# Output tiles 0 to 3 of an attention and FFN kernel emitted in another order

## The chip, the cores and the metric

The kernel runs on all 8 cores of one Trainium2 chip, each core on two of the 16 sequences, with no exchange between cores. The time is device microseconds of the slowest core, and smaller is better. Engines: PE does matrix products, DVE elementwise work and statistics, ACT the exponentials, POOL (GpSimd) elementwise work in SBUF, SP issues DMAs. Each takes its instructions strictly in the order in which the program gave them out.

## What is computed

```python
# x: (16, 2048, 1024); 16 heads of 64
x = x + ln(attn(ln(x)))     # q = xWq; k = (xWk)Wl; v = (xWv)Wl; softmax(q k^T / 8) v; then Wo, bo
x = x + ln(ffn(ln(x)))
def ffn(x):                 # base + shared low rank + routed low rank
    base = x @ base_W.T + base_b
    shared = (x @ shared_A.T) @ shared_B.T                    # rank 16
    gate = softmax(x @ router_W.T + router_b)                 # 6 experts, top 2, renormalised
    h = einsum('bsi,eri->bser', x, routed_A)
    routed = einsum('bser,eor,bse->bso', h, routed_B, sparse(gate))
    return base + shared + routed
```

## The kernel before

A core's work is one main loop of 512 steps m (`for m in range(NM)`, below `def rate_of`). A step issues two score blocks (`qk(2m)`, `qk(2m+1)`), then a portion of side work for PE from the list `filler`, then the two products of the probabilities with v of the step before (`pv`). ACT makes one exponential of 128x1024 for each score block. Steps 0 to 255 are the attention of sequence 0, 256 to 511 that of sequence 1. Four steps make a unit: at its end, in steps divisible by four, DVE gets a reciprocal (L1171) and a product (L1183).

`filler` is a flat list of (cost, function, ready). One cost unit is about one 128x128 by 512 matmul. The list is taken strictly from its head. In each step `credit` grows by `rate` and is capped at 1.6 times the rate; items are issued while credit is positive and the head's `ready` holds. An item that isn't ready holds back everything behind it, and what credit goes beyond the cap is lost. For m below 256 the rate is 6.03 units (1,496 units in 248 steps); from 256 on it is what is left of the list divided by the steps up to m = 481, about 4.5 to 4.6.

The input projections of both sequences fill the list up to m = 247. Then come the 32 output tiles of 128 rows. A tile n has these links:

- `tr_u(n)` (2 units): 8 PE transpositions of the attention output into a PSUM bank `fb`, and one DVE copy to `ut` (L251).
- `z_group(n, h)`, h = 0, 1 (8 units each): the product with Wo. At the end of each half DVE adds the bias (L812) and takes statistics (L257); after h = 1 also L261, and POOL runs the chain of `norm_add`: three operations on 128x1 (L266 to L268), a scale of 128x1024 (L277), an add of 128x1024 (L793).
- `ln3(n)` (no PE work), not before 3 steps after z: two DVE statistics and L261, which need POOL's add, then on POOL L266 to L268 and the scale into `xn` (L277).
- `tr3(n)` (2 units), not before 3 steps after `ln3`: 8 transpositions (L853) and a DVE copy to `x3fm`.
- `h_group(n)` (1.84 units): the low-rank product with the router's columns. DVE copies it to `hs` (L868), adds the router's bias (L870), takes the maximum; two steps later ACT takes the exponentials.
- `gate_a(n)`, `gate_b(n)`: DVE alone, six and six small operations (L890 to L896, L903 to L910).
- `tr_h(n)` (0.25 unit): one transposition (L924) of the gated `hm`, and a copy.
- `y_group(n, h)` (9 units each): the FFN's product, with DVE and POOL work at its end as for z (L946, L257, L261, then POOL's chain and the store).

So a tile is some 40 units. The filler matmuls have two PSUM banks, handed out by `next_bank`:

```python
if len(ring["list"]) == 2 and not big:
    return ring["list"][ring["n"] % 2]
b = ring["list"][ring["n"] % len(ring["list"])]
ring["n"] += 1
```

A half of z or y is `big` and moves the ring on. A transposition or an `h_group` is not: it takes the bank that the next half will get, and leaves the ring as it is. Each group waits on PE, before its first matmul, until DVE has emptied its bank (`bfree`). For `h_group` that is the copy L868, for a transposition the copy L251.

The order of the tiles is written out in the loop `for n in range(NT - 2)` (L992). In the pass for tile n, `tr_u(n+1)` and `gate_a(n-2)` lie inside z(n, 0), `tr3(n-1)` and `gate_b(n-2)` inside z(n, 1), then y(n-2) with `tr_h(n-2)` and `h_group(n-1)` inside its first half and `ln3(n)` inside its second. For n = 0 and 1 there is no y. Tiles 28 to 31 have an order of their own.

Of the kernel before, what the change touches and what calls it, by code (L numbers as in the profile page):

```python
# [70 lines left out]
def build_nc():  # L71
# [17 lines left out]
    with ExitStack() as ctx:  # L89
# [503 lines left out]
        def add(fn, cost=0.0, ready=None):  # L593
            filler.append((cost, fn, ready))
# [6 lines left out]
        def past(name, dm):  # L601

            return lambda: state["tail"] or name in mark and clock["m"] >= mark[name] + dm

        def held(group, ready):
            return [(group[0][0], group[0][1], ready)] + group[1:]
# [143 lines left out]
        def u_ready(n):  # L750
            if n >= NT - 2:
                return n in u_last and clock["m"] >= u_last[n][1] + 1
            return (n // 2 in u_tok and len(u_tok[n // 2][1]) == (8 if n < 16 else 1)
                    and clock["m"] >= u_tok[n // 2][2] + 1)

        def load_u(n):

            if n < NSEQ * 16 - 2:
                seq, t = tile_of(n)
                done_at(("l", n))  # L760
                u_ld[n] = P.dma("Y", qur[n % 2], urow[n % 2][:], u_scr[seq, t], u_tok[n // 2][1],
                                urow_free[n % 2], fb_tok["a1"])
# [44 lines left out]
        def z_group(n, h):  # L807
            s, xs = n % 2, n % 4

            def evict(pa, tok):  # L810
                o = x2[xs][:, h * 512:(h + 1) * 512]
                ev = P.op("V", lambda v: v.tensor_tensor(o, pa, bo_t[:, h * 512:(h + 1) * 512], ALU.add),  # L812
                          tok, bo_evs, x2_free[xs] if h == 0 else None, fb_tok["a1"])
                a = ln_stats("z", n % 4, h, o, ev)
                if h == 1:
                    u_free[s] = tok
                    ag = ln_aggr("z", n % 4, a)
                    slot, xt = res[n]

                    def done(tok2, half):  # L820
                        z_out[n] = xload["free"][slot] = tok2
                        if half is not None:
                            z_half.append(tok2)
                    norm_add(n, "z", x2[xs], xst[slot], ag, done, xt)
                    done_at(("z", n))
                return ev
            return late_group(512, lambda k: ut[s][:, k, :], lambda k: wo_sb[:, k, h * 512:(h + 1) * 512],
                              NCH, evict, lambda: [ut_tok[n], w_tok["wo"]])
# [4 lines left out]
        def ln3(n):  # L833
            xs, s = n % 4, n % 2
            done_at(("x", n))
            ln_stats("x", n % 4, 0, x2[xs][:, 0:512], z_half[0] if n == NT - 1 else z_out[n])
            a = ln_stats("x", n % 4, 1, x2[xs][:, 512:1024], z_out[n])
            ag = ln_aggr("x", n % 4, a)
            rt = ln_rstd("x", n % 4, ag)
            xn3_tok[n] = ln_apply("S" if n == NT - 1 else "G", "x", n % 4, xn3[s][:], x2[xs][:], rt, xn3_free[s],  # L840
                                  fb_tok["a1"])
# [131 lines left out]
        def t3_of(n):  # L973
            return [(2.0, lambda: tr3(n), past(("x", n), 3))]

        def h_of(n):
            return held(h_group(n), past(("t", n), 1))

        def th_of(n):
            return [(0.25, lambda: tr_h(n), past(("gb", n), 1))]  # L980
# [8 lines left out]
            else:  # L989
                add(lambda: gate_b(n), 0.0, past(("ga", n), 1))  # L990

        for n in range(NT - 2):  # L992
            tu = [(2.0, lambda n=n: tr_u(n + 1), past(("l", n + 1), 2))] if n + 1 < NT - 2 else []
            z0 = held(z_group(n, 0), past(("u", n), 1))
            filler += z0[:4] + ([] if late(n + 1) else tu) + z0[4:6]
            if n > 1:
                gates(n - 2, 0)
            filler += z0[6:]
            if n + 2 < NT - 3:
                if not late(n + 2):  # L1000
                    add(lambda n=n: load_u(n + 2), 0.0, lambda n=n: u_ready(n + 2))
            elif late(n + 1):
                at_late.append(len(filler))
                add(lambda n=n: load_u(n + 1), 0.0, lambda n=n: u_ready(n + 1))
                add(lambda n=n: load_u(n + 2), 0.0, lambda n=n: u_ready(n + 2))
            z1 = z_group(n, 1)
            filler += z1[:4] + (t3_of(n - 1) if n > 0 else []) + z1[4:6]
            if n > 1:
                gates(n - 2, 1)
            filler += z1[6:]  # L1010
            h = h_of(n - 1) if n > 0 else []
            if n > 1:
                y0, y1 = y_of(n - 2, 0), y_of(n - 2, 1)
                filler += y0[:2] + th_of(n - 2) + y0[2:6] + h + y0[6:] + y1[:4] + (tu if late(n + 1) else [])
            else:
                filler += h
                y1 = []
            filler += y1[4:6]
            add(lambda n=n: ln3(n), 0.0, past(("z", n), 3))
            filler += y1[6:]  # L1020
# [319 lines left out]
```

How the kernel before makes its waits and increments, by code:

```python
    def wait(self, e, *toks):  # L40
        for tok in toks:
            if tok is None:
                continue
            if isinstance(tok, list):
                self.wait(e, *tok)
                continue
            sem, val = tok
            key = id(sem)
            if self.seen[e].get(key, 0) < val:
                self.seen[e][key] = val
                self.q[e].append(lambda eng, h=sem[0], v=val: eng.wait_ge(h, v))
# [1 line left out]
    def op(self, e, fn, *toks):  # L53
        self.wait(e, *toks)
        sem = self.sem[e]
        sem[1] += 1
        self.q[e].append(lambda eng, fn=fn, h=sem[0]: fn(eng).then_inc(h, 1))
        return (sem, sem[1])
# [5 lines left out]
    def dma(self, e, sem, out, in_, *toks):  # L64
        self.wait(e, *toks)
        sem[1] += 16
        self.q[e].append(lambda eng, o=out, i=in_, h=sem[0]: eng.dma_start(out=o, in_=i).then_inc(h, 16))
        return (sem, sem[1])
```

## Time and profile before

| | us |
|---|---|
| median of 3 runs | 1413.39 (1412.29 to 1520.67) |
| the profiled execution | 1412.82 |
| span of its slowest core (core 4) | 1411.3 |
| spans of the eight cores | 1407.9 to 1411.3 |

The profile is of core 4. The span is from its first to its last instruction; 1.5 us of the run lie around it. Busy time says where an engine worked. Idle time of PE, with what ended it, says what PE waited for. The clock is given as granted share of full speed. Names with numbers left out (`fb`, `ut`, `xn`) are the buffers above; `x` as an output of L812, L277 and L793 is the buffer `x2`.

### The profile page before, as it was taken

What the parts mean: (1) busy time and instruction counts of PE and PEld (TensorE: products, weight loads), DVE (VectorE), ACT (ScalarE), POOL (GpSimd) and SP (SyncE); (2) the same over time, 40 slices, a digit from 0 to 9 for tenths busy, and PEclk for the clock granted to TensorE, in tenths of its full rate; (3) what the DMA queues carried; (4) which work ended last, traced back from release to release, by engine and by line L of the source; (5) the groups of instructions that cost most, each with busy time, mean ns of one, the idle gap of its engine ahead of it and who ended that gap; (6) DMA issues with size and microseconds to landing.
All of it is one profiled execution on the core that took longest, in us unless ns stands there. A gap on an engine that the chain in (4) does not pass through costs nothing.

```text
span 1411.3 us, 43965 instructions; the slowest of 8 cores (1407.9 to 1411.3 us)
## 1 busy us (share of the span) xinstructions
PE 1317.9 (93%) x17392; PEld 818.0 (58%) x17392; DVE 705.3 (50%) x1679; ACT 1042.0 (74%) x1138; POOL 433.5 (31%) x598
## 2 busy tenths in 40 slices
PE   6899999999999999999998999989999999998883
PEld 2456666666666666665555655555555555555551
DVE  0562434323332323232335676677777667667665
ACT  0367777777777777777777888878888888887651
POOL 5220101000010100000004555555556555465633
PEclk9999999999999999999999999999999999999997
DMA  9950112202020110123852212321222221222011
GB/s 131 232 162 6 54 30 73 64 17 59 15 62 19 47 43 26 25 78 92 113 114 64 77 59 72 121 71 60 77 78 82 91 77 45 86 69 86 23 62 45
DMA packets 67129, 98.90 MB, mean 70 GB/s; under 512 B 30208, under 2 KB 43904, under 8 KB 66416
## 3 DMA queue, kind: packets, MB, share of 16 engines
q1 hardware_dynamic: 56944, 83.03, 19.5%
q0 software_dynamic: 9984, 13.06, 6.8%
q8 instruction: 142, 2.33, 0.7%
q14 instruction: 59, 0.48, 0.1%
HBM read 76.56 MB, written 32.57 MB: 77 GB/s over the span
## 4 chain that ended last, share of the span: by engine, by line
PE 76%; DVE 7%; issue 5%; ACT 5%; DMA 3%; POOL 2%; DVEq 0%; SPq 0%; POOLq 0%; ACTq 0%
PE fb L379 34%; PE sc L1122 17%; PE av L1154 15%; ACT p_sb L1139 4%; PE fb L431 4%; DMA wvT_sb<-wvT 2%; DVE gt L896 1%; PE sc L379 1%; DVE x L812 1%; PE fb L853 1%; DMA xst<-x 1%; PE fb L776 1%; PE sc L1124 1%; POOL wl_sb L67 1%; PE fb L324 1%
## 5 line engine op out<-in xcount | busy, mean ns | idle before, releaser
L1139 ACT ACTIVATE p_sb<-sc 128x1024 bf16<-128x1024 f32 x1024 | 991.0, 1021 | 261.3 <-PE sc L1124 258.2
L1154 PEld LDWEIGHTS av<-v_sb,p_sb 128*128 128x128 bf16 x8192 | 320.8, 97 | 97.1 <-issue 2.3
L1122 PE MATMUL sc<-q_sb,k_sb 64*128 64x256 bf16 (+1 forms) x2176 | 330.6, 265 | 16.0 <-ACT p_sb L1139 14.5
L1154 PE MATMUL av<-v_sb,p_sb 128*128 128x65 bf16 x8192 | 340.1, 193 | 0.5 <-issue 0.5
L1124 PE MATMUL sc<-q_sb,k_sb 64*128 64x256 bf16 (+1 forms) x2176 | 332.8, 266 | 0.0
L1122 PEld LDWEIGHTS sc<-q_sb,k_sb 64*128 64x128 bf16 x2176 | 149.6, 94 | 82.8 <-issue 46.8
L266 POOL TENSOR_SCALAR rsa<-sta 128x1 f32<-128x1 f32 x32 | 7.3, 227 | 523.9 <-DVE sta L261 357.4
L1124 PEld LDWEIGHTS sc<-q_sb,k_sb 64*128 64x128 bf16 x2176 | 146.3, 94 | 0.0
L379 PE MATMUL fb<-wo_sb,ut 128*128 128x512 bf16 x496 | 136.1, 381 | 4.9 <-DVE gt L890 3.3
L379 PE MATMUL fb<-bw_sb,x3fm 128*128 128x512 bf16 x480 | 135.6, 383 | 1.0 <-DVE x3fm L251 0.9
L379 PE MATMUL fb<-xfm,wq_sb 128*128 128x512 bf16 x512 | 129.5, 381 | 0.0
L379 PE MATMUL fb<-xfm,wkl_sb 128*128 128x512 bf16 x480 | 123.5, 381 | 0.0
L251 DVE CAST v_sb<-fb 128x512 bf16<-128x512 f32 (+3 forms) x52 | 33.3, 640 | 94.0 <-PE fb L431 52.7
L379 PEld LDWEIGHTS fb<-xfm,wq_sb 128*128 128x128 bf16 x512 | 43.6, 98 | 55.7 <-issue 17.1
L793 POOL TENSOR_TENSOR x<-x,xst 128x1024 f32<-128x1024 f32 x31 | 73.0, 2355 | 6.5 <-POOL x L277 6.5
L793 POOL TENSOR_TENSOR y_sb<-y_sb,x 128x1024 f32<-128x1024 f32 x31 | 72.9, 2352 | 4.6
L379 PEld LDWEIGHTS fb<-xfm,wkl_sb 128*128 128x128 bf16 x480 | 40.5, 98 | 53.1 <-issue 19.4
L379 PEld LDWEIGHTS fb<-wo_sb,ut 128*128 128x128 bf16 x496 | 39.4, 97 | 54.8 <-issue 28.2
L244 DVE TENSOR_SCALAR k_sb<-fb,bklc 128x512 bf16<-128x512 f32 x45 | 33.8, 751 | 72.8 <-PE fb L379 72.4
L379 PEld LDWEIGHTS fb<-bw_sb,x3fm 128*128 128x128 bf16 x480 | 39.9, 99 | 45.9 <-issue 19.2
L379 PE MATMUL fb<-wvl_sb,xfm 128*128 128x512 bf16 x256 | 64.7, 381 | 0.0
L266 POOL TENSOR_SCALAR rsz<-stz 128x1 f32<-128x1 f32 x32 | 7.3, 227 | 185.4 <-DVE hT L251 84.0
(172 smaller groups left out, 1478.5 us busy)
## 6 DMA issues: line engine op xcount, KB each, us to landing
xst<-x SPq DMA_DIRECT2D x64, 512.0 KB, 5.2
out<-y_sb SPq DMA_DIRECT2D x31, 512.0 KB, 3.1
urow<-u_scr SPq DMA_DIRECT2D x30, 256.0 KB, 5.2
u_scr<-u SPq DMA_DIRECT2D x64, 64.0 KB, 2.1
q_scr<-kq SPq DMA_DIRECT2D x32, 128.0 KB, 2.5
q_sb<-q_scr SPq DMA_DIRECT2D x4, 1024.0 KB, 8.3
u_scr<-u_sb SPq DMA_DIRECT2D x7, 512.0 KB, 3.6
wkT_sb<-wkT POOLq DMA_DIRECT2D x8, 256.0 KB, 11.6
```

Of the source, the lines that this page charges most:

```text
L67: self.q[e].append(lambda eng, o=out, i=in_, h=sem[0]: eng.dma_start(out=o, in_=i).then_inc(h, 16))
L244: return P.op("V", lambda v: v.tensor_scalar(out, ps, col, scale, ALU.add, ALU.mult), *toks)
L251: return P.op("V", lambda v: v.tensor_copy(out, ps), *toks)
L266: a = P.op("G", lambda g: g.tensor_scalar(r_[:, 0:1], s_[:, 13:14], EPS, None, ALU.add), tok)
L324: r = t.transpose(pb[:, c * 128:(c + 1) * 128], xn[xs][:, c * 128:(c + 1) * 128], identb[:])
L379: r = t.matmul(pa, lhs(k), rhs(k), start=(k == 0), stop=(k == nk - 1))
L431: r = t.matmul(pa[:, tt * 128:(tt + 1) * 128], xfm[sl][:, k, tt * 128:(tt + 1) * 128], wvl_sb[:, k, j * 128:(j + 1) * 128], start=(k == 0) ...
L793: done(P.op("G", lambda g: g.tensor_tensor(out[:], out[:], x[:], ALU.add), yt, *toks), None)
L1122: t.matmul(sc[slot][:, ci * w:(ci + 1) * w], k_sb[0:64, j, c * 128:(c + 1) * 128], qa[0:64], start=True, stop=True, tile_position=(0, 0))
L1124: r = t.matmul(sc[slot][:, 512 + ci * w:512 + (ci + 1) * w], k_sb[64:128, j, c * 128:(c + 1) * 128], qa[64:128], start=True, stop=True, ti ...
L1139: exp_tok[g] = P.op("S", lambda a: a.activation(ps[:], sc[slot][:], AF.Exp, bias=-SHIFT, scale=1.0), tok, av_tok.get(g - 4))
L1154: r = t.matmul(av[u % 2][:, o:o + 65], ps[:, p0:p0 + 128], v_sb[:, j, c * 130 + h * 65:c * 130 + (h + 1) * 65], start=(s == 0 and h == 0 a ...
```

## The change

The loop now begins at n = 4, and tiles 0 to 3 are written out ahead of it. The operations and their number stay the same; only the order changes, and with it the steps in which the items fall. z(0) to z(3) come in front, each followed by `tr_u(n+1)` at its end and not inside the next z. `ln3(n-1)` follows z(n). `tr3(0)` lies between z(2) and `ln3(1)`, with `h_group(0)` behind them; `tr3(1)` inside z(3). Then the gates of tile 0 around `h_group(1)`, y(0), the gates of tile 1, y(1), with `tr3(2)`, `tr_h` and `h_group(2)` between.

```diff
-        for n in range(NT - 2):
+
+        for n in range(4):
+            if n > 0:
+                add(lambda n=n: load_u(n + 1), 0.0, lambda n=n: u_ready(n + 1))
+            z0, z1 = held(z_group(n, 0), past(("u", n), 1)), z_group(n, 1)
+            tu = [(2.0, lambda n=n: tr_u(n + 1), past(("l", n + 1), 2))]
+            filler += z0 + z1[:4] + (t3_of(1) if n == 3 else []) + z1[4:] + tu
+            if n > 1:
+                filler += t3_of(0) if n == 2 else []
+                add(lambda n=n: ln3(n - 1), 0.0, past(("z", n - 1), 3))
+                filler += h_of(0) if n == 2 else []
+            elif n == 1:
+                add(lambda: ln3(0), 0.0, past(("z", 0), 3))
+        add(lambda: load_u(5), 0.0, lambda: u_ready(5))
+        gates(0, 0)
+        filler += h_of(1)
+        gates(0, 1)
+        y0, y1 = y_of(0, 0), y_of(0, 1)
+        filler += y0[:4] + th_of(0) + y0[4:]
+        add(lambda: ln3(3), 0.0, past(("z", 3), 3))
+        filler += y1[:4]
+        gates(1, 0)
+        filler += y1[4:] + t3_of(2)
+        gates(1, 1)
+        y0, y1 = y_of(1, 0), y_of(1, 1)
+        filler += y0[:2] + th_of(1) + y0[2:6] + h_of(2) + y0[6:] + y1
+        for n in range(4, NT - 2):
```

## Rows read from the trace of the kernel before

**Rows 1.** The page: busy us of each engine (share of the span) x instructions
```profile
PE 1317.9 (93%) x17392; PEld 818.0 (58%) x17392; DVE 705.3 (50%) x1679; ACT 1042.0 (74%) x1138; POOL 433.5 (31%) x598
```
**Rows 2.** Three stretches: length, busy time of each engine (instructions), granted clock, DMA
```profile
480.00:728.00 248.00, 247.69 (x3251) 156.07 (x3249) 78.54 (x153) 195.55 (x202) 12.33 (x20) 1.00 0.34 64
728.00:771.00 43.00, 36.29 (x505) 22.17 (x502) 20.56 (x54) 31.56 (x35) 15.07 (x22) 1.00 0.33 95
771.00:1280.00 509.00, 483.32 (x6631) 293.28 (x6629) 348.81 (x923) 420.91 (x480) 284.65 (x347) 1.00 0.23 74
```
**Rows 3.** The chain that ended last, near 692 us: start, duration, what
```profile
691.16 1.40 PE fb L379 x6
692.56 0.50 PE av L1154 x16
...
693.60 1.40 PE fb L379 x6
```
**Rows 4.** What PE waited for, 728 to 771: total us, times, longest
```profile
PE sc L1122 <- ACT p_sb L1139: 3.4, 7, 0.5
PE fb L379 <- DVE rT L1171: 1.2, 1, 1.2
PE fb L379 <- DVE gt L890: 1.2, 1, 1.2
```
**Rows 5.** Timeline of ACT, first starved steps: start, duration, engine [idle before]
```profile
736.47 5.61 ACT L1139 ACTIVATE p_sb<-sc 128x1024 bf16<-128x1024 f32 x6 [0.29 <-PE sc L1124]
```
**Rows 6.** Timeline of DVE: the statistics of ln3(0)
```profile
743.06 1.29 DVE L257 BATCH_NORM_STATS2 stx<-x 128x6 f32<-128x512 f32 x2 [5.61 <-POOL x L793]
```
**Rows 7.** Timeline of PE and DVE at the end of z(0)
```profile
735.38 0.66 PE L1154 MATMUL av<-v_sb,p_sb 128*128 128x65 bf16 x16
...
735.65 0.69 DVE L812 TENSOR_TENSOR x<-fb,bo_t 128x512 f32<-128x512 f32 x1 [0.90 <-PE fb L379]
...
737.24 0.21 DVE L261 BATCH_NORM_AGGREGATE stz<-stz 128x2 f32<-128x12 f32 x1
```
**Rows 8.** Timeline of DVE and PE: a copy of ut, and the matmul behind it
```profile
728.02 0.69 DVE L251 COPY ut<-fb 128x1024 bf16<-128x1024 bf16 x1 [0.30 <-PE av L1154]
...
728.86 0.81 PE L379 MATMUL fb<-wo_sb,ut 128*128 128x512 bf16 x3 [0.33 <-DVE ut L251]
```
**Rows 9.** Timeline of DVE: a copy to hs behind other work
```profile
752.62 0.26 DVE L868 COPY hs<-fb 128x118 f32<-128x118 f32 x1
...
753.52 0.15 DVE L873 TENSOR_SCALAR gt<-gt 128x1 f32<-128x1 f32 x1
```
**Rows 10.** Timeline of POOL: first and last operation of the chain behind a z
```profile
789.03 0.23 POOL L266 TENSOR_SCALAR rsz<-stz 128x1 f32<-128x1 f32 x1 [4.34 <-DVE hT L251]
...
791.99 2.35 POOL L793 TENSOR_TENSOR x<-x,xst 128x1024 f32<-128x1024 f32 x1 [0.21 <-POOL x L277]
```
**Rows 11.** Timelines of POOL, DVE and PE, 820 to 828: gates beside POOL's chain
```profile
820.37 1.19 POOL L277 TENSOR_SCALAR y_sb<-y_sb,rsy 128x1024 f32<-128x1024 f32 x1 [0.18 <-POOL rsy L268]
821.71 2.34 POOL L793 TENSOR_TENSOR y_sb<-y_sb,x 128x1024 f32<-128x1024 f32 x1
...
821.04 0.53 DVE L891 TENSOR_TENSOR gt<-gt 128x1 f32<-128x1 f32 x1
...
822.01 2.06 DVE L896 CAST gt<-gi 128x2 f32<-128x2 uint32 x1
...
824.82 0.61 PE L853 MATMUL fb<-identb,xn 128*128 128x128 bf16 x8 [1.26 <-DVE x L812]
...
826.49 0.28 DVE L903 TENSOR_SCALAR gt<-small_sb,gt 128x6 f32<-128x6 f32 x1
...
827.67 0.26 DVE L910 TENSOR_TENSOR hm<-hs,gt 128x96 bf16<-128x96 f32 x1
```
**Rows 12.** What PE waited for, 771 to 1280
```profile
PE fb L853 <- DVE x L812: 11.3, 9, 1.7
PE fb L924 <- DVE x L812: 3.5, 6, 1.0
```

## Prediction

> **What bounds the kernel now.** I read the page first: PE is busy for 93% of the span and ACT for 74% [rows 1], so PE bounds the loop as long as it is fed. Then the busy times by stretch, around the place that the change touches. From 480 to 728 us, with projections as side work, PE idles 0.31 us in 248. From 728 to 771, where tiles 0 to 2 start, it idles 43.00 - 36.29 = 6.7 us in 43. From 771 to 1280 it idles 25.7 us in 509, or 0.5 in 10. The granted clock is 1.00, the 2.4 GHz level, in all three [rows 2]. The change can win at most those 6.7 us in the second stretch, 0.5% of the time, and what else it may win or lose lies in the waits of the third.
>
> The chain gives a step's price: 1.40 us for six filler matmuls, hence 0.22 a unit at that price (0.23 at most), and 693.60 - 692.56 = 1.04 us for two pv and two qk [rows 3]. A step without side work lasts as long as two exponentials: six took 5.61 us, so 1.87 a step [rows 5], of which PE idles 0.83. A step of 2 units idles 0.39, one of 4 nothing.
>
> I then walked the list through the credit rule and checked the walk against the timeline. It puts z(0) into steps 251 to 253, leaves 254 and 255 empty because `ln3(0)` at the head must wait three steps, and has short steps at 258 (2 units), 260 (1.84), 261 (0) and 264 (2). The trace has the same steps. Their cost is 0.83 x 3 + 0.4 x 3 = 3.7 us, near the 3.4 us in which PE waited for ACT [rows 4]. The other 2.4 us are two waits of 1.2 behind DVE [rows 4]: `ln3(0)` is issued three short steps after z(0), before POOL's add is done, DVE stands still for 5.61 us [rows 6], and the copy and the evictions behind it come late. The same occurs for `ln3(1)`.
>
> **What the change takes away.** By the walk of the new list (starting credit as the trace has it), z(0) now takes 251 to 253, z(1) 254 to 256, z(2) 257 to 260, z(3) 262 to 265. No step is empty, and 13 more units are issued before step 256. Two steps are short, 261 and 271, with 2 units each. `ln3(0)` comes at 257, 4 steps after z(0), when POOL is done. So nearly all of the 6.7 us would go, if nothing came in their place. Loads move by two steps at most, in a stretch with a DMA share of 0.33 [rows 2]; each `load_x` reuses a slot freed two or more tiles earlier, so SP is not held, and nothing queued behind it is. I cost them at nothing.
>
> **What it adds.** The new order puts a short, non-big item directly behind the end of a group and ahead of a group that gets the same bank. DVE works in order, so the short item's copy stands behind the big eviction.
>
> (a) A z ends on PE at 735.38. DVE's eviction begins at 735.65 and the last of three operations ends at 737.45, 2.07 us after PE [rows 7]. A copy to `ut` takes 0.69, and the matmul behind it starts 0.15 later, at 728.86 [rows 8]. With an overlap of 0.1 between DVE operations that makes 2.8 us after the z's end. PE needs 0.45 for the transpositions and 1.04 for pv and qk, so it stands there after 1.5. The wait is 1.3 us. Before, `tr_u` sat inside the next z, four units behind the eviction, and the wait was covered. It now comes at the starts of z(1), z(2) and `tr3(0)` (this last behind `tr_u(3)`, same bank, and POOL's `xn(0)` is ready about then), and at `h_group(1)` behind `tr_u(4)`, where the boundary lies ahead of the transposition: four times. It comes again at y(1, 0), behind `tr3(2)` which now follows y(0): a fifth.
>
> (b) z(3) follows `h_group(0)` and needs its bank. DVE has the copy `x3fm(0)` and the two statistics of `ln3(1)`, 1.29 us [rows 6], before `hs(0)`, 0.26 [rows 9]. That again gives 2.8 against 1.5: a sixth wait of 1.3. Together 7.8 us.
>
> (c) The dearest. `ln3(2)`, `gate_a(0)`, `h_group(1)` fall in step 266, right after z(3). Let t be the end of DVE's L261 of z(3), 2.1 us after z(3) ends on PE. POOL's chain starts at t + 0.1; its add begins 2.96 later and ends 5.31 after the start [rows 10], and L277 runs in the 1.34 us before the add [rows 11]. DVE does `ut(4)`, the statistics of `ln3(2)`, and reaches L891 at t + 2.4, inside L277. What happens then, a pair of rows shows: L891 lasted 0.53 until L277 ended, 0.45 later L896 began, 0.3 into the add, and lasted 2.06 until the add was over [rows 11]. L873, an operation as small, takes 0.15 [rows 9]. So DVE is free at t + 5.4, `hs(1)` is copied by t + 5.7, and y(0, 0), which gets that bank, starts at t + 5.8, or 7.9 after z(3)'s end. PE is there after 2.8 + 0.45 + 1.04 = 4.3. The wait is 3.6 us. Queued behind it on PE are all later qk and pv, so ACT stands too.
>
> (d) `tr_h(0)` needs `gate_b(0)`, which is behind `hs(1)`, its router operations (0.9 [rows 9]) and 1.44 of its own [rows 11], to 10.1 or, if it meets `ln3(2)`'s L277, 10.7. PE is there at 7.9 + 0.87 + 1.04 = 9.8: 0.3 to 0.9, I take 0.7. `tr_h(1)` in step 272 meets y(0)'s chain in the same way, 0.8.
>
> The sum of the new waits is 7.8 + 3.6 + 0.7 + 0.8 = 12.9 us. With the copy of `ut(0)` (0.33, in both) and the usual short waits for ACT, 0.5, it is 13.7. Against 6.7 gone, PE's idle time grows by 7.0. The bounds: below, the copies might slip into DVE's gaps, each of the six waits be 0.8 and (c) not meet the add (then 0.5), so 6.8 us and no change; above, each 1.6 and (c) another add behind the first, 17, so +11.
>
> The Trainium skill (SBUF — State Buffer, SBUF: two separate sides) has for this that VectorE and GpSimd hold a shared pair of ports for a whole instruction, and the other fully blocks; VectorE only in a two-port mode or with two SBUF inputs. The trace agrees for L891 and L896 [rows 11]. By that rule it is a lock on single instructions, and (c) is as priced; if both merely slowed each other, L896 would end earlier and (c) would be some 2 us less. It speaks against this order.
>
> **The later tiles.** Nine times between 771 and 1280 PE waited at `tr3` for an eviction, 11.3 us in all, 1.26 each, and six times at `tr_h`, 3.5 us [rows 12]. The nine are the tiles whose L896 lasted over 2 us, as in [rows 11]. Whether gates meet the add depends on where steps fall: in those nine, two boundaries lie between the end of y(n-1) and `tr_u`, or a unit's end on DVE lies between `tr_u` and the gates, or just ahead of them. The new list has 4.53 units a step where the old had 4.60, so the pattern shifts. Sorted in the same way, tiles 2 to 24 give nine to ten meetings. I take +0.6 us, with 4 us on either side.
>
> **Sum.** Core 4's run was 1412.82, of which 1411.3 is span. 1412.8 + 7.0 + 0.6 = 1420.4. The undisturbed runs shown are 1412.29 and 1413.39, around the profiled one, so I say 1420.
>
> **The rivals.** A: new waits as above, 1420; its own range 1415 to 1426. Chance 0.64. B: the reorder does what it looks like: the short items' copies are in time, the 6.7 us shrink to 1 or 2, and the time is 1408. For it: the empty steps do go, that is certain from the list. Against: rows 7 and 8 leave no room for a `ut` copy within 1.5 us. Chance 0.14. C: a near draw, 1411 to 1415, when (c) misses the add and the later pattern is kinder. 0.14. D: slower by far: gates meet the add in all of tiles 3 to 24, not nine. That is 13 more meetings at 1.26 and as many waits at `tr_h` near 0.6, so 24 us on top of A, 1444. It decides, against 2%, from about 12 more meetings on; the phase moves with every tile (40.1 units at 4.53 a step is 8.85 steps), which speaks against it. A few more than nine is likelier, and the rest of D's 0.08 is there, 1426 to 1432. The full 24 gets 0.01.
>
> **Numbers.** The range 1410 to 1426 leaves out B's centre and D: 0.2. Within 2%, about what a measurement of this kernel can tell from no change, is 1385 to 1442. A, B and C lie inside: same 0.98, slower 0.01, faster 0.01. The likeliest is a small loss all the same.
>
> **What would show it.** PE timeline 728 to 780: no step without filler (if there is one, the walk is wrong). Waits of 1.3 before the first matmul of z(1) and z(2), ended by the copy of `ut` (a). One of 3 to 4 us before y(0, 0) with L896 of some 2 us ahead of `hs` (c). PE idle near 14 us up to y(1), where now 6.7. Later: nine or ten L896 above 2 us. Wrong it would be if DVE's copies came within 1.5 us of a group's end, or if POOL's add were over before `gate_a(0)`.

## The result

| | before | after |
|---|---|---|
| median of 8 runs each, us | 1412.96 (1411.72 to 1520.67) | 1426.26 (1423.71 to 1577.1) |
| slowest core of the profiled execution, us | 1411.3 | 1424.7 |
| fourth fastest core in it, us | 1409.7 | 1419.6 |
| core 4 in it, us | 1411.3 | 1418.1 |

After to before is 1.009, with a 95% interval of 1.0078 to 1.0103. The change costs 13.3 us, inside the 2%. The forecast was 1420, from 1410 to 1426; the median lies 0.3 us above that range, and the loss is 1.75 times the 7.6 us forecast. Some executions of every kernel take 1 to 11% longer, and the ratios here and below leave out those over 1.5% above the fastest (before 1435.98 and 1520.67, after 1487.4, 1574.4 and 1577.1).

Lines of this section are of core 4, as those before the prediction were. Columns are as in [rows 2]. Of a few groups the trace lacks the record of the first matmul; the row then starts 0.2 to 0.4 us late, and its wait is too long by as much.

Stretches of the kernel after:
```profile
728.00:771.00 43.00, 37.41 (x514) 23.18 (x511) 21.57 (x43) 30.68 (x35) 18.28 (x23) 1.00 0.45 117
...
771.00:785.00 14.00, 9.68 (x117) 5.87 (x114) 10.20 (x28) 7.77 (x11) 6.87 (x9) 0.88 0.01 1
```
PE idles 43.00 - 37.41 = 5.6 us in the stretch where it had idled 6.7 [rows 2], and then 4.3 us more in 14. The same times do not hold the same steps any more, so I compare by steps. The "clock of step m" is the time at which ACT starts the first exponential of step m, read from ACT's timeline on each core. Between steps 250 and 290 stand all the moved items. Before, they took 96.85 us, with PE busy for 88.82. After:
```profile
728.66:837.31 108.65, 92.65 (x1253) 56.81 (x1249) 69.01 (x165) 78.31 (x88) 49.06 (x63) 0.98 0.26 75
```
These are 11.8 us more: 8.0 of idle time (16.00 against 8.03) and 3.8 of busy time. Of the busy time, 12.25 filler units are work that comes earlier and is given back later, 2.7 us at 0.22 a unit. The rest, 1.1 us, is a lower clock, here 0.98 against 1.00.

What PE waited for, first up to 785 us and then up to step 290 (total us, times, longest):
```profile
PE fb L379 <- DVE hs L868: 3.7, 2, 3.2
PE fb L379 <- DVE ut L251: 2.3, 3, 1.0
PE fb L776 <- DMA urow<-u_scr: 1.4, 1, 1.4
PE fb L379 <- DVE rT L1197: 1.4, 1, 1.4
PE sc L1148 <- ACT p_sb L1165: 1.0, 4, 0.5
...
PE fb L379 <- DVE x3fm L251: 2.2, 1, 2.2
PE fb L853 <- DVE x L812: 1.9, 2, 1.0
PE sc L1148 <- ACT p_sb L1165: 1.3, 6, 0.4
PE fb L924 <- DVE x L812: 0.5, 1, 0.5
```
The short waits for ACT of the empty steps are mostly gone up to 785 us, 3.4 us [rows 4] against 1.0. In their place stand long waits behind DVE. Each of them is one matmul at the head of a group, on PE's timeline (start, duration, what, [idle before, what ended it]):
```profile
740.02 1.67 PE L379 MATMUL fb<-wo_sb,ut 128*128 128x512 bf16 x7 [1.03 <-DVE ut L251]
...
748.91 1.02 PE L379 MATMUL fb<-wo_sb,ut 128*128 128x512 bf16 x4 [1.38 <-DVE rT L1197]
...
757.76 0.61 PE L776 MATMUL fb<-identb,urow 128*128 128x128 bf16 x8 [1.45 <-DMA urow<-u_scr]
...
762.84 1.24 PE L379 MATMUL fb<-wo_sb,ut 128*128 128x512 bf16 x5 [0.54 <-DVE hs L868]
...
773.58 0.59 PE L379 MATMUL fb<-astk_sb,x3fm 128*128 128x118 bf16 x8 [0.94 <-DVE ut L251]
...
778.41 1.06 PE L379 MATMUL fb<-bw_sb,x3fm 128*128 128x512 bf16 x4 [3.20 <-DVE hs L868]
...
791.23 0.59 PE L379 MATMUL fb<-bw_sb,x3fm 128*128 128x512 bf16 x2 [2.22 <-DVE x3fm L251]
```
These are, in order, z(1), z(2), `tr_u(3)`, z(3), `h_group(1)`, y(0, 0) and y(1, 0). On six of the eight cores z(1), z(2), `h_group(1)`, y(0, 0) and y(1, 0) wait for the same times to within 0.02 us, and on the other two (0 and 6) once the missing matmuls are allowed for. The load before `tr_u(3)` is the exception: 0.83 to 2.34 us on five cores and nothing on cores 2, 6 and 7, where `tr3(0)` waits 1.0 instead, and z(3) then 1.0 and not 0.54. The largest is y(0, 0), and DVE's and POOL's timelines show what stood ahead of `hs(1)`:
```profile
774.32 1.19 POOL L277 TENSOR_SCALAR x<-x,rsz 128x1024 f32<-128x1024 f32 x1 [0.18 <-POOL rsz L268]
775.72 2.34 POOL L793 TENSOR_TENSOR x<-x,xst 128x1024 f32<-128x1024 f32 x1 [0.21 <-DVE gi L892]
...
775.11 0.41 DVE L891 TENSOR_TENSOR gt<-gt 128x1 f32<-128x1 f32 x1
...
775.97 2.11 DVE L896 CAST gt<-gi 128x2 f32<-128x2 uint32 x1
...
778.00 0.27 DVE L868 COPY hs<-fb 128x118 f32<-128x118 f32 x1
```
L891 is held until L277 ends (774.32 + 1.19 = 775.51). L896, two elements a partition, begins 0.25 us into POOL's add and ends with it (775.72 + 2.34 = 778.06). Only then can `hs(1)` be copied, and y(0, 0) starts 0.14 us after that copy.

At y(1, 0) POOL has no part. `xn(2)` is ready at 780.99, and PE transposes it at 787.36 without a wait. DVE is late (its timeline):
```profile
785.94 1.27 DVE L257 BATCH_NORM_STATS2 stx<-x 128x6 f32<-128x512 f32 x2
...
788.35 0.69 DVE L946 TENSOR_TENSOR y_sb<-fb,bb_t 128x512 f32<-128x512 f32 x1
...
790.39 0.69 DVE L251 COPY x3fm<-fb 128x1024 bf16<-128x1024 bf16 x1 [0.24 <-issue]
```
The statistics of `ln3(3)` and all of `gate_a(1)` stand between 785.94 and 788.44 and hold up the eviction of y(0, 1); the copy of `x3fm(2)` comes behind that.

The later loop is the same in sum. From step 290 to step 480, PE idled 24.3 us before (822.90 to 1274.98) and 25.0 after:
```profile
837.31:1287.44 450.13, 425.15 (x5835) 257.96 (x5833) 307.82 (x799) 372.63 (x424) 246.05 (x301) 1.00 0.22 74
```
The waits in it, from 840 to 1285 us, are these:
```profile
PE sc L1148 <- ACT p_sb L1165: 11.2, 58, 0.4
PE fb L853 <- DVE x L812: 9.4, 10, 1.3
PE fb L924 <- DVE x L812: 2.8, 5, 0.7
```
In the same steps before, `tr3` and `tr_h` had the 11.3 and 3.5 us of [rows 12], and the waits for ACT came to 7.8. So the waits for DVE are 2.6 us less and those for ACT 3.4 more, where 11 units of filler fewer are left for these steps.

### The profile page after: what moved, and what is told of

Read it like the earlier page. It is cut to its first block, busy times and chain, and to the rows that moved or that the text cites. A ratio compares the mean times of both kernels' runs of the same rounds, so it can differ in the third digit from the quotient of the medians.

```text
span 1424.7 us, 43962 instructions; the slowest of 8 cores (1418.1 to 1424.7 us)
## 1 busy us (share of the span) xinstructions
PE 1325.3 (93%) x17392; PEld 822.2 (58%) x17392; DVE 712.8 (50%) x1679; ACT 1042.6 (73%) x1138; POOL 432.3 (30%) x598
## 4 chain that ended last, share of the span: by engine, by line
PE 75%; DVE 8%; issue 6%; ACT 6%; DMA 3%; POOL 1%; SPq 0%; DVEq 0%; ACTq 0%; POOLq 0%
PE fb L379 34%; PE sc L1148 16%; PE av L1180 15%; ACT p_sb L1165 5%; PE fb L431 4%; DMA wvT_sb<-wvT 2%; PE sc L379 2%; DVE gt L896 1%; DVE x L812 1%; PE fb L853 1%; PE fb L776 1%; PE sc L1150 1%; DVE gt L891 1%; PE av L379 1%; PE fb L324 1%
## 5 line engine op out<-in xcount | busy, mean ns | idle before, releaser
L1148 PEld LDWEIGHTS sc<-q_sb,k_sb 64*128 64x128 bf16 x2176 | 151.0, 94 | 82.6 <-issue 45.9
L1150 PEld LDWEIGHTS sc<-q_sb,k_sb 64*128 64x128 bf16 x2176 | 147.9, 94 | 0.0
```

Of the source, the lines that this page charges most:

```text
L1148: t.matmul(sc[slot][:, ci * w:(ci + 1) * w], k_sb[0:64, j, c * 128:(c + 1) * 128], qa[0:64], start=True, stop=True, tile_position=(0, 0))
L1150: r = t.matmul(sc[slot][:, 512 + ci * w:512 + (ci + 1) * w], k_sb[64:128, j, c * 128:(c + 1) * 128], qa[64:128], start=True, stop=True, ti ...
```

## The experiments

The table gives the step clocks of each kernel against the kernel before: the median over the eight cores of the difference, set to 0 at step 250, in us. Positive is later than before. Some filler work stands earlier or later in the one than in the other, so the differences at steps 256 to 290 hold up to about 3 us of work that is given back by step 480. The last column is the measured time over that of before on the same chip. The kernels ran on several chips. After ran on the first and, as f0, on another, and its step clocks agree to 0.2 us, so the clocks of the other kernels are set against it too.

| kernel | 256 | 260 | 262 | 268 | 272 | 290 | 480 | ratio (95%) |
|---|---|---|---|---|---|---|---|---|
| after | +2.7 | +1.4 | +2.7 | +6.5 | +9.7 | +13.0 | +11.3 | 1.0090 (1.0078 to 1.0103) |
| after, again (f0) | +2.7 | +1.4 | +2.6 | +6.5 | +9.5 | +13.1 | +11.3 | 1.0094 (1.0057 to 1.0131) |
| e1_tr_inside | | -1.0 | +1.6 | +5.5 | +9.4 | +12.5 | +10.8 | 1.0074 (1.0058 to 1.0090) |
| e2_small_add | | | +2.6 | +2.9 | +6.4 | +9.7 | +8.0 | 1.0045 (1.0029 to 1.0061) |
| e3_gate_early | | | | +5.8 | +8.0 | +10.2 | +8.6 | 1.0065 (1.0049 to 1.0081) |
| f2_tr3_inside | | | | +6.4 | +10.7 | +14.0 | +13.0 | 1.0093 (1.0079 to 1.0107) |

The first question was which of the new waits carries how much, and whether the lock of POOL's add on small DVE operations is what makes y(0, 0) wait.

**The add made small.** The changed order, with the scale and the add of z(3)'s chain on 8 of 1024 columns. It leaves out the norm and the residual of tile 3 in the other 1016.

```diff
-                yt = ln_apply("G", kind, n % 4, out[:], out[:], rt)
-                done(P.op("G", lambda g: g.tensor_tensor(out[:], out[:], x[:], ALU.add), yt, *toks), None)
+                w = 8 if (kind, n) == ("z", 3) else D
+                yt = ln_apply("G", kind, n % 4, out[:, 0:w], out[:, 0:w], rt)
+                done(P.op("G", lambda g: g.tensor_tensor(out[:, 0:w], out[:, 0:w], x[:, 0:w], ALU.add), yt, *toks), None)
```

> The changed order; POOL's scale and add behind z(3) cover 8 of the 1024 columns, so tile 3 of the first sequence lacks its first norm and residual in the rest. DVE's work and its order are untouched. Theory 1 (L891 and L896 are held by POOL's running operation): L896 of gate_a(0) falls from 2.1 to 0.15 us, the wait before y(0,0) from 3.2 to about 1.0, and with it the low clock near 775 to 785 goes, worth 1.7 to 3.4 us: in all 4 to 6 us, 1420 to 1422. Rival (DVE is simply late by the length of its queue, POOL does not matter): 3.2 us stay and the time is 1426. Second rival (the clock fell for another reason than this wait): the wait shrinks, the low clock stays, 1424.

It took 1418.07 us, against 1411.48 for before on that chip. DVE's timeline, and then PE's, core 4 (the lines are numbered one higher than in after):
```profile
771.90 0.15 DVE L897 CAST gt<-gi 128x2 f32<-128x2 uint32 x1
771.96 0.28 DVE L869 COPY hs<-fb 128x118 f32<-128x118 f32 x1
...
772.60 0.81 PE L379 MATMUL fb<-bw_sb,x3fm 128*128 128x512 bf16 x3 [1.21 <-DVE lg L871]
```
The same instruction takes 0.15 us and not 2.11. The wait before y(0, 0) falls from 3.20 to 0.99: core 4's row says 1.21, with one matmul unrecorded, and the six cores with whole records say 0.99. Step 268 comes 3.6 us earlier than in after. So POOL's two operations are what held it, the add above all. At step 480 the gain is 3.3 us, of 4 to 6 expected. The stretch of low clock behind y(0, 0) is gone on all eight cores, but five have one behind y(1, 0), which still waits 2.2; and PE now waits 0.85 before `tr_h(0)`, where it waited for nothing in after.

**The gates early.** Undoing the meeting by order alone: `gate_a(0)` two units before the end of z(3), ahead of POOL's chain.

```diff
-            filler += z0 + z1[:4] + (t3_of(1) if n == 3 else []) + z1[4:] + tu
+            filler += z0 + z1[:4] + (t3_of(1) if n == 3 else []) + z1[4:6]
+            if n == 3:
+                gates(0, 0)
+            filler += z1[6:] + tu
...
-        gates(0, 0)
```

> The changed order with gate_a(0) moved from behind tr_u(4) into the last quarter of z(3,1), before POOL's chain of that tile begins. Theory 1: gate_a(0) meets nothing, hs(1) is copied at once, the wait before y(0,0) falls to some 0.3 us; but L870 and gate_b(0) now come while the add of z(3) runs, so tr_h(0) waits some 2.3 us. Together 0.6 to 1 us less waiting, and as the stall is split in two, the low clock may go: 1422 to 1425. If it were the length of DVE's queue alone, both waits would be below 0.5 us and the time 1421.

It took 1420.77 us, 2.6 less than after at step 480. The wait at y(0, 0) fell to 1.09, where 0.3 was expected, and `gate_b(0)`, which comes next, ran into the same add (POOL's, DVE's and PE's timelines, core 4):
```profile
770.95 2.34 POOL L793 TENSOR_TENSOR x<-x,xst 128x1024 f32<-128x1024 f32 x1 [0.21 <-DVE lg L870]
...
771.20 2.12 DVE L903 TENSOR_SCALAR gt<-small_sb,gt 128x6 f32<-128x6 f32 x1
...
774.63 0.23 PE L924 MATMUL fb<-identb,hm 128*112 128x128 bf16 x1 [2.11 <-DVE hm L910]
```
L903 takes 0.28 elsewhere [rows 11] and 2.12 here. It ends at 773.32, the add at 773.29. The next small operation behind the one that is moved away inherits the block, and it costs no less there: 1.09 and 2.11 are the 3.20 of after, in two parts. What is gained lies elsewhere. y(1, 0) waits 1.50 and not 2.22 (with 0.46 new at `tr_h(1)`), and there are fewer stretches of low clock, one on six of the cores where six had two. Core 4 has one in both, and from step 262 to step 290 it loses 8.17 us to before here and 8.93 in after.

**The transpositions inside the next z.** This undoes part (a) alone, as the old order had it.

```diff
-            if n > 0:
-                add(lambda n=n: load_u(n + 1), 0.0, lambda n=n: u_ready(n + 1))
...
-            filler += z0 + z1[:4] + (t3_of(1) if n == 3 else []) + z1[4:] + tu
+            filler += z0[:4] + tu + z0[4:]
+            add(lambda n=n: load_u(n + 2), 0.0, lambda n=n: u_ready(n + 2))
+            filler += z1[:4] + (t3_of(1) if n == 3 else []) + z1[4:]
```

> The changed order, with one thing put back: tr_u(n+1) lies four units into z(n, 0) and the load of u for tile n+2 goes out right after that half, so no transposition stands between two z. Theory 1 (a short item's copy stands behind the big eviction on DVE): the waits of 1.03 us before z(1), 1.38 before z(2) and 0.94 before h_group(1) go; the 1.45 us for the load of urow before tr_u(3) goes too, since the load leaves one step earlier. Together 4.8 us, so about 1421 instead of 1426. The 3.2 us before y(0,0) and the low clock behind it stay. Rival (POOL's chain of 8.7 us a tile is what holds the four z): the waits only move to tr3(0) and tr3(1), and the time stays at 1426.

It took 1421.31 us. That is the number expected and not for the reason expected, since after itself took 1421.80 on another chip (f0, below). The waits at z(1), z(2) and for the load are gone: step 260 comes 2.4 us earlier than in after. Then `tr3(0)` waited for POOL (POOL's and PE's timelines, core 4):
```profile
750.58 0.23 POOL L266 TENSOR_SCALAR rsx<-stx 128x1 f32<-128x1 f32 x1
...
752.98 1.19 POOL L277 TENSOR_SCALAR xn<-x,rsx 128x1024 bf16<-128x1024 f32 x1 [0.72 <-PE fb L379]
...
754.43 0.61 PE L853 MATMUL fb<-identb,xn 128*128 128x128 bf16 x8 [2.15 <-DVE stz L261]
...
773.89 1.86 PE L379 MATMUL fb<-bw_sb,x3fm 128*128 128x512 bf16 x4 [4.00 <-DVE hs L868]
```
`ln3(0)`'s normalisation is queued on POOL behind the whole chain of z(1), since POOL too works in order. `xn(0)` ends at 754.17 and PE starts 0.26 later. The wait at y(0, 0) grew to 4.00, and at step 480 only 0.4 us are left of the 2.4. The waits of (a) are real but largely cover one for POOL behind them.

**The last transposition moved on.** `tr3(2)` goes from between y(0) and y(1) into y(1, 0), to take away the wait of 2.2 us at y(1, 0).

```diff
-        filler += y1[4:] + t3_of(2)
+        filler += y1[4:]
...
-        filler += y0[:2] + th_of(1) + y0[2:6] + h_of(2) + y0[6:] + y1
+        filler += y0[:2] + t3_of(2) + th_of(1) + y0[2:6] + h_of(2) + y0[6:] + y1
```

> The changed order with tr3(2) moved two units into y(1,0), from between y(0,1) and y(1,0). Theory 1: y(1,0) then no longer needs the bank of tr3(2), whose copy x3fm stands behind the eviction and two statistics of y(0,1); its wait of 2.2 us goes, nothing takes its place, and as it falls into the second stretch of low clock on most cores, up to another 1.45 us go with it: 2.2 to 3.6 us faster than the changed kernel. Rival (POOL or the gates hold this place anyway): the wait moves to tr_h(1) or to tr3(2) itself, and the gain is below 0.7 us.

It took 1424.67 us, against 1421.80 for the changed kernel on the same chip. The wait came back one item later, and a little longer (PE's timeline, core 4):
```profile
789.04 0.23 PE L924 MATMUL fb<-identb,hm 128*112 128x128 bf16 x1 [2.65 <-DVE x3fm L251]
```
`tr_h(1)` now stands directly behind `tr3(2)` and gets its bank, so it needs the copy of `x3fm(2)`. On DVE that copy is given out behind `gate_b(1)`: the gate runs from 786.66 to 788.30 and the copy from 788.21 to 788.89, while PE had done `tr3(2)` by 786.4. At step 480 it is 1.7 us behind after, where 2.2 to 3.6 us were to be gained. The new place only exchanged one short neighbour in the same bank for another.

The second question was whether the gain that the order seems to offer, the empty steps of [rows 4], can be had at all. These kernels keep the four projections in front and pull the short items apart, so that each stands inside a projection or an FFN group and not between two.

**Spread.** The head rewritten; its core:

```diff
+        filler += z0[:4] + tu_of(1) + z0[4:]
...
+        filler += z1[:5]
+        x_of(0)
+        filler += z1[5:]
...
+        filler += z1[:4] + t3_of(0) + z1[4:]
+        z0, z1 = held(z_group(3, 0), past(("u", 3), 1)), z_group(3, 1)
+        filler += z0[:2]
+        x_of(1)
+        filler += z0[2:4] + h_of(0) + z0[4:6] + tu_of(4) + z0[6:]
+        ld(5)
+        filler += z1[:3] + t3_of(1) + z1[3:6]
+        gates(0, 0)
+        filler += z1[6:]
...
+        filler += y0[:4]
+        gates(0, 1)
+        x_of(2)
+        filler += y0[4:6] + h_of(1) + y0[6:7] + th_of(0) + y0[7:] + y1[:4]
```

> Tiles 0 to 3 in an order by theory 1: every transposition and h_group stands two or more units inside a half of z or y, never at its end; ln3(0) is issued inside z(1,1), ahead of POOL's chain of z(1); gate_a(0) inside z(3,1), gate_b(0) four units into y(0,0). No step is without side work, two are short (2 units). Theory 1: PE idles 3 to 5 us in the stretch where before idles 6.7 and the change about 14, and the clock stays up: 1409 to 1412, just ahead of before. Rival (the 13 units issued before step 256 are not given back, because later steps are short enough to wait for ACT, 12.5 instead of 9.2 us there): 3 us more, 1412 to 1415, no gain over before.

It took 1410.36 us, inside the 1409 to 1412 expected, ratio 0.9997 (0.9971 to 1.0024): the whole loss is gone, and no gain that can be told from none. By the step clocks it is 2.4 us ahead of before at step 264, 0.2 behind at 266 and 4.1 behind at 290, with 12.25 units given out early as in after, and 1.4 ahead at 480. PE's and POOL's timelines, core 4, show the place:
```profile
763.95 0.61 PE L853 MATMUL fb<-identb,xn 128*128 128x128 bf16 x8 [2.27 <-POOL xn L277]
...
755.53 0.23 POOL L266 TENSOR_SCALAR rsz<-stz 128x1 f32<-128x1 f32 x1 [2.28 <-DVE stz L261]
...
760.95 0.23 POOL L266 TENSOR_SCALAR rsx<-stx 128x1 f32<-128x1 f32 x1
...
762.50 1.19 POOL L277 TENSOR_SCALAR xn<-x,rsx 128x1024 bf16<-128x1024 f32 x1 [0.18 <-POOL rsx L268]
```
`xn(1)` stands behind z(2)'s chain on POOL, which runs from 755.53 to 760.9, and a lower clock follows at 763 on every core.

**Spread, with ln3(1) ahead of z(2)'s chain.** The only difference to the last one is where `ln3(1)` stands. The last one was run again beside it.

```diff
-        filler += z1[:4] + t3_of(0) + z1[4:]
...
-        filler += z0[:2]
+        filler += z1[:4] + t3_of(0) + z1[4:5]
         x_of(1)
-        filler += z0[2:4] + h_of(0) + z0[4:6] + tu_of(4) + z0[6:]
+        filler += z1[5:]
...
+        filler += z0[:4] + h_of(0) + z0[4:6] + tu_of(4) + z0[6:]
```

> The first spread order with one link moved: ln3(1) goes out inside z(2,1), five units earlier, so that POOL makes xn(1) before the chain of z(2) and not behind it. All other items keep their steps, so the later tiles keep their pattern. Theory 1: the wait of 2.3 us before tr3(1) goes, and with it the 3.4 us at the lower clock near 763 (1.45 us): 3 to 4 us faster than the first spread order, 0.996 to 0.998 of before. Rival (a wait removed here comes back at the next link, as when tr3(2) was moved): less than 1 us.

> The first spread order again, on the chip of the kernel beside it, as its reference: by its first run 1.000 of before, or 1 us less.

They took 1409.03 and 1410.00 us (medians), against 1411.88 for before; the ratios are 0.9978 (0.9918 to 1.0038) and 0.9975 (0.9919 to 1.0030). These intervals do not separate the two from each other, nor from before. They are wide because the counted times fall into two groups, one at 1425 to 1430 in all three kernels. The lower groups are 1406.9 to 1409.0 for this one (seven executions, median 1407.2), 1407.8 to 1410.1 for the last one (seven, 1409.2) and 1409.7 to 1413.3 for before (thirteen, 1411.3). Sorted so, which was not planned, this one is 4.1 us or 0.3% ahead of before with no overlap, and 2 us ahead of the last one. The traces show the difference on the place itself: the step clocks against before at 264, 268, 290 and 480 are -2.0, -2.2, +1.6 and -3.9 for this one, where the last one has -1.4 at step 480. What PE waited for from 728 to 840, core 4:
```profile
PE sc L1168 <- ACT p_sb L1185: 3.0, 15, 0.4
PE fb L853 <- DVE x L812: 1.3, 2, 1.0
```
No wait for POOL is left, and no lower clock. The gain over the last one is 2.5 us at step 480, of 3 to 4 expected. This is the fastest order found, 0.2 to 0.3% below before by its medians.

Little of that lead comes from the moved items. From step 250 to 290 PE idles 6.6 us, 1.4 less than before. From 290 to 480 it idles 22.3, and 2.0 less than before's 24.3: the waits at `tr3` and `tr_h` of the later tiles, whose order is the same, come to 9.4 us and not 14.8 (seven L896 above 2 us, where before had nine), and those for ACT to 10.7 and not 7.8. The new head shifts the steps in which the later tiles fall, and this shift seems to be a good one.

**No short steps at all.** One further step from the last one: `tr_u(5)` into y(0, 0), `gate_b(0)` and `h_group(1)` earlier, `gate_b(1)` ahead of `tr3(2)`, so that every step up to 290 has 3 units or more. `h_group(0)` and `ln3(3)` move by a few units too.

```diff
-        filler += y0[:4]
+        filler += y0[:3]
         gates(0, 1)
+        filler += y0[3:4] + h_of(1) + y0[4:5]
         x_of(2)
-        filler += y0[4:6] + h_of(1) + y0[6:7] + th_of(0) + y0[7:] + y1[:4]
+        filler += th_of(0) + y0[5:7] + tu_of(5) + y0[7:] + y1[:4]
...
```

> The spread order, second version. Of the first, tr3(1) waited 2.3 us for POOL, since ln3(1) was issued behind z(2) and POOL did the chain of z(2) first; after that the clock was low for 3.4 us on all cores, and three steps were short. Now ln3(1) is issued inside z(2,1), tr_u(5) fills a gap in y(0,0), gate_b(1) comes ahead of tr3(2), and no step has under 3 units. Theory 1: the 2.3 us and the low clock (1.45 us) go, 1 us of short steps too: 3 to 5 us faster than the first version, 1405 to 1407, and 0.996 to 0.998 of before. Rival (units issued early come off steps that then wait for ACT): the gain is half of that, 1408.

It took 1412.46 us, 1.0006 (0.9996 to 1.0015), where 1405 to 1407 was expected. It led by 2.3 us at step 268, but the lead was gone at 274 (+1.2), and it was 2.0 behind at 290. Two waits of its own stand there in the 728 to 840 stretch, core 4:
```profile
PE fb L924 <- DVE x3fm L251: 1.4, 1, 1.4
PE fb L776 <- DVE hT L251: 1.4, 1, 1.4
```
Both are short items one or two units behind another in the same bank. `tr_u(5)` needs the copy `hT` of `tr_h(0)`, which stands on DVE behind the statistics of `ln3(2)`; `tr_h(1)` needs the copy of `x3fm(2)`, which stands behind `gate_b(1)`.

But at step 290 this kernel is only 0.5 us behind the last one. At step 480 it is 4.7 behind (+0.9 against -3.9), with the same 12.25 units given out early. The rest is lost in the later tiles, which but for `tr_u(5)` have the same order in both. PE idles 22.3 us from step 290 to 480 there, and 25.7 here (the last one's row, then this one's, core 4):
```profile
824.55:1271.64 447.09, 424.81 (x5835) 258.10 (x5833) 303.27 (x799) 372.70 (x424) 246.62 (x302) 1.00 0.23 74
...
820.96:1271.80 450.84, 425.19 (x5835) 258.23 (x5833) 307.73 (x799) 372.91 (x424) 246.02 (x301) 1.00 0.22 74
```
The waits at `tr3` and `tr_h` are 9.4 us in the one and 13.0 in the other, with seven L896 above 2 us and nine. A few units' shift at the head goes with 3.4 us of idle time in the tiles behind it. That the shift is the cause is argued and not shown: no run here varies it alone.

**The changed kernel on another chip.** To see how much of the first difference belongs to the cores.

> The changed kernel unaltered, on the chip of this group, so that its neighbours are compared with it and not with a figure from another chip. Every theory: 1.009 of before, so some 1424; PE's waits the same, one or two stretches of 3.4 us at the lower clock on each core between 770 and 795 us, and the slowest core 3 to 5 us above the fourth slowest.

It took 1421.80 us against 1411.23, so +10.6, where the first chip showed +13.3 and 1424 was expected. The ratio of the medians is 1.0075; the 1.0094 of the table holds one execution of 1439.17. The step clocks agree with those of after to 0.2 us (table). What differs is how far the slowest core stands from the rest. In the median over its runs on the first chip it is at 1424.7 and the fourth core at 1419.6; here they are at 1420.2 and 1418.0. Before has 1411.3 and 1409.7 in the first profile, 1409.7 and 1407.6 here. So the fourth core lost 9.9 and 10.4 us on the two chips, and about 3 of the 13.3 us are the lag of one core.

## Why the prediction was right, and where its sizes were off

**The walk: right.** The step at which each item falls is as forecast, on every step from 251 to 272; no step is empty, and the two short ones are 261 and 271. The gain of the 6.7 us did come.

**(a) and (b), six waits of 1.3: the mechanism is right, the sizes are not even.** They measured 1.03 at z(1), 1.38 at z(2), 0.54 at z(3), 0.94 at `h_group(1)` and 2.22 at y(1, 0), and nothing at `tr3(0)`. In sum they are 6.1 against 7.8. The one at `tr3(0)` was hidden on core 4 behind a wait that the forecast had at nothing; on the three cores without that wait it is there, with 1.0. For z(3) the forecast says that its operations "again" give 2.8 us and adds nothing up; it is the least of the six. At y(1, 0) it left out what DVE has ahead of the eviction, `ln3(3)` and `gate_a(1)`.

**The loads: wrong.** `tr_u(3)` waited 1.45 us for its `urow`. I had argued from the DMA share of the stretch, 0.33, and from the slots, which are indeed free. What I left out is the queue: the load is now wanted at step 260 and not 262, and SP has eight loads of the next heads in front of it, as before had (SP's timeline, core 4):
```profile
746.95 1.75 SPq L67 DMA_DIRECT2D k_sb<-k_scr  x4
748.74 2.29 SPq L67 DMA_DIRECT2D v_sb<-v_scr  x4
...
751.54 0.47 SPq L67 DMA_DIRECT2D urow<-u_scr  x1
```
They hold SP for 4.1 us, and the transfers then fill the DMA engines. A mean over the stretch (0.33 before, 0.45 after) hides a part at 0.88:
```profile
748.00:760.00 12.00, 9.47 (x135) 6.00 (x136) 6.87 (x15) 7.75 (x9) 7.95 (x13) 1.00 0.88 231
```
e1, whose load leaves at 734.88, ahead of the eight, did not wait for it. On three cores of after the load came in time, so the 1.45 us is one core's value and not the kernel's.

**(c), 3.6 us at y(0, 0): right.** It measured 3.20 (3.19 to 3.21 on the six cores with whole records), by the instructions named: L891 held by L277, then L896 by the add. e2 shows that it is the add. The Trainium skill (SBUF — State Buffer, SBUF: two separate sides) calls this a lock for the whole instruction and no sharing of bandwidth. The runs agree: L896 (778.08 against 778.06) and, in e3, L903 (773.32 against 773.29) end with the add, though alone they take 0.15 and 0.28.

**(d), 0.7 and 0.8 at `tr_h`: the first hidden, the second wrong.** Both measured 0. For `tr_h(0)` the mechanism is there all the same: DVE's L910 takes 0.90 us and not 0.26, as L277 of `ln3(2)` runs until 780.99, and `tr_h(0)` starts at 781.24, 0.15 after L910's end. PE had only just got there, because its clock was low from 779.3 on (below). By its times at full clock, 0.87 and 1.04 after 778.41, it would have stood there at 780.3 and waited 0.9, an estimate; in e2, at full clock, it waits 0.85. The second was to come from gates that meet y(0)'s chain on POOL. They do not meet it (L903 takes 0.28 there), and what is late at that place is the copy of `x3fm(2)`, behind other work on DVE, for which y(1, 0) pays with 2.22 where 1.3 was forecast.

**The sum.** The waits named come to 9.3 us, and with the load's to 10.8, where 12.9 was forecast. The idle time from step 250 to 290 nevertheless grew by 8.0 and not 7.0. The forecast compared up to y(1), and up to there PE idles 12.1 us, near the 14 it named. The difference lies beyond y(1): 1.9 us at `tr3` and 0.5 at `tr_h` fall between it and step 290, where before had only waits for ACT and 0.3 at `tr_h`. From 290 on another 0.7 came. Together +8.7 against the forecast +7.6, a miss of 1 us.

**The later tiles: right in size, partly by luck.** The forecast was nine or ten L896 above 2 us and +0.6 us. In after eleven are, from 785 to 1285, where before had nine (two of the eleven lie ahead of step 290), and the idle time from step 290 to 480 grew by 0.7. But that sum is made up otherwise than forecast: the waits at `tr3` and `tr_h` are 2.6 us less, and those for ACT 3.4 more. Rival D, that all tiles would meet the add, falls.

**What was missed: the clock.** The forecast took it at 1.00 throughout. After the long wait it is at its lower level, 1.2 GHz, for a stretch (after, core 4):
```profile
779.00:782.40 3.40, 3.40 (x31) 2.04 (x29) 2.10 (x8) 1.80 (x4) 1.58 (x3) 0.54 0.02 5
```
In it the 16 matmuls of an `av` group take 1.08 us on PE's timeline, and 0.66 at full clock [rows 7]. Core 4 has this one alone. Of the others six have two such stretches of about 3.4 us each between 740 and 800 us (in three of them one directly behind the other), and core 5 has three; before, six cores have none there and two have one. Its price can be read in e2, whose cores wait equally long at y(0, 0), `tr_h(0)` and y(1, 0), once missing records are allowed for. Between steps 262 and 290, three of them (0, 1, 7) have no such stretch and lose 6.04 to 6.08 us to before; the five with one lose 7.44 to 7.61. That makes 1.4 to 1.5 us each. g0 says the same at another place: core 1, without a stretch there, loses 2.88 us over these steps, and the seven with one 4.19 to 4.47. Here is e2's core 0, and then core 3, from 771 to 795:
```profile
771.00:795.00 24.00, 19.77 (x278) 12.68 (x279) 15.96 (x54) 16.57 (x21) 10.12 (x17) 1.00 0.06 24
...
771.00:795.00 24.00, 19.77 (x261) 12.28 (x257) 14.31 (x53) 16.00 (x21) 9.67 (x15) 0.93 0.06 24
```
Core 3 is busy for as long as core 0 and gets 261 matmuls done instead of 278. Two stretches would make 2.9 us, which is most of what the forecast lacks at step 480 on the median core: 11.3 there, 7.6 forecast, 1 in waits. That it follows from the long waits is shown as far as this: it begins during one of them or at most 1.5 us behind it, e3, without the wait of 3.2, has one on most cores, f2, with its wait of 2.65, has two or three, and f1 and g1, without a wait over 2 us, have none in this region. It doesn't follow each time: in e2 three cores wait 2.2 at y(1, 0) and have none behind it, in g0 one waits 2.27 and has none. What decides that stays open.

**The slowest core.** From step 480 on, 0.9 us is given back (+10.4 at step 511, median core). What takes that to 13.3 us is one core of the first chip, which ends later than the rest by 3 us more than in before; f0 does not show it. A forecast from one core's trace has no term for it.

**Rivals B and C** fell: the copies were not in time, and (c) did meet the add. But B's idea can be had in another order: g1 keeps the projections in front, has no empty steps and none of the long waits. It comes to 1409.0, where B had 1408. The empty steps were worth little: [rows 4] gives 3.4 us at most, and of g1's lead 1.4 us of idle time lie in the moved items' steps and 2.0 in the later tiles'.

## What to carry to other kernels

Where side work is fed to an engine in groups, put a short item that shares the groups' banks inside a group, some units behind the last eviction, never between two groups: its copy queues behind that eviction, and the head of the next group, with all that is behind it, stands. For the same reason don't let two short items that get the same bank follow each other closely. Follow each in-order queue (DVE, POOL, and the one that issues loads) through the new order, not only the sum of work, and look for small DVE operations that fall into a long GpSimd one: the cost is that of the long operation, and it goes to whatever is next if the small one is merely moved. A wait of 2 to 3 us in an otherwise full loop has a price beyond itself, since the clock may fall behind it. And look at the unchanged part behind the change too: here it came out 2 us better in one kernel and 1 us worse in another.

## What the runs showed of the hardware

A wait of 3.2 us of PE was followed by 3.4 us at the lower clock, at 1.4 to 1.5 us a stretch. Waits of 2.2 us had one on five of eight cores in e2, and of 2.27 on seven of eight in g0. In before, with waits of up to 1.2 us there, six of eight cores had none. The Trainium skill (TensorE: Matmul & The Clock Gate, Part 1: The HAM clock gate) gives two levels, 1.2 and 2.4 GHz; the rows agree, with a granted 0.50 to 0.54 and 1.00. That page of the Trainium skill also expects 13/16 of the full clock with three or more cores of a die on dense matmuls. Here all eight are, with PE busy for 93%, and mostly the granted clock stands at 1.00 [rows 2]. But that level occurs too, on some cores and for some of the time: in g0's profiled execution cores 6 and 7 were granted 0.81 for 160.4 us (from 57.5 us on), and they took 1427.0 and 1424.1 us where the other six took 1403.8 to 1407.7. So the measurements have it as an exception and not as the rule.

POOL's add of 128x1024 held small DVE operations until its end: a cast of 128x2 took 2.11 us in after and 0.15 in e2, an operation of 128x6 2.12 in e3 and 0.28 elsewhere.

The cores do not start step 250 together. In the other ten profiled executions they lie between 5.5 us ahead of the same core in before and 4.0 behind it, with the same work up to there (g0's cores 6 and 7 apart, which are 16 and 17 behind). The time of the kernel is that of the last of them, so by these numbers 2 to 3 us of a difference between two kernels can be this alone, and a comparison by step clocks on each core, set to zero ahead of the change, is sharper than the times.
